# A graph network kernel: node one-hots of the end tiles made by one compare per 125 nodes over all neighbouring tiles of a side

## The reference: what is computed

```python
def _L1_gnn_ref(x, edge_index, W_interact, b_interact, W_update, b_update):
    src, dst = (edge_index[0], edge_index[1])
    h_edge = jnp.concatenate([x[src], x[dst]], axis=-1)
    m_ij = jax.nn.relu(h_edge @ W_interact + b_interact)
    m_i = jax.ops.segment_sum(m_ij, src, num_segments=x.shape[0])
    m_i = m_i / jnp.asarray(math.sqrt(AVG_DEGREE), dtype=x.dtype)
    out = x + jax.nn.relu((x + m_i) @ W_update + b_update)
    return out
```

## Time and profile before

| | |
|---|---|
| median of 3 runs | 1886.35 us (1883.08 to 1886.48) |
| span of the profiled execution | 1885.1 us, 1.25 us under that median |
| PE busy | 1694.0 us, 90% |
| DVE busy | 1432.5 us, 76% |
| ACT busy | 1037.5 us, 55% |
| POOL busy | 1024.9 us, 54% |
| edge stage | 1116 to 1885 us |

### The profile page before, as it was taken

The page is one execution under the profiler, slowest core; times in us unless marked ns, Lnnn a source line. Parts: engine busy times, 40 slices in busy tenths (PEclk is TensorE's granted clock), DMA queues, the critical chain, the costliest instruction groups (busy, mean ns, idle before and its releaser), DMA issues.

```text
span 1885.1 us, 45388 instructions
## 1 busy us (share of the span) xinstructions
PE 1694.0 (90%) x16778; PEld 1472.1 (78%) x16778; DVE 1432.5 (76%) x5527; ACT 1037.5 (55%) x2015; POOL 1024.9 (54%) x1075
## 2 busy tenths in 40 slices
PE   1606798999999979999999759999999999999998
PEld 1403676888778757777777649999999999999998
DVE  7968998999998335676653558888787777887776
ACT  1715575666667450000000248877777777777776
POOL 3364105656551004566551157777777777777775
PEclk9955999999999999999999879999999999999998
DMA  3005526465553656666666223443443444444442
GB/s 99 1 1 169 211 114 217 151 220 192 178 218 116 255 188 253 238 244 240 239 240 227 59 72 104 104 111 107 123 114 104 112 111 105 111 107 122 115 105 71
DMA packets 135014, 276.48 MB, mean 147 GB/s; under 512 B 21160, under 2 KB 82393, under 8 KB 134794
## 3 DMA queue, kind: packets, MB, share of 16 engines
q1 hardware_dynamic: 98427, 201.82, 31.1%
q0 software_dynamic: 34784, 71.17, 14.2%
q10 hardware_dynamic: 1584, 0.59, 0.1%
HBM read 192.26 MB, written 84.45 MB: 147 GB/s over the span
## 4 chain that ended last, share of the span: by engine, by line
PE 45%; DVE 24%; POOL 16%; issue 8%; DMA 4%; ACT 1%; POOLq 1%; SPq 1%; DVEq 0%
PE ps L1111 23%; POOL cells L810 8%; DVE hot L1595 7%; PE ps L1284 6%; PE ps L1277 5%; PE ps L1295 4%; POOL cell_lo L810 3%; POOL cell_hi L810 3%; DVE hot L1589 3%; PE ps L1097 2%; PE ps L1144 2%; DMA cells<-b_rows,work 2%; DVE keys L1685 1%; DVE keys L1619 1%; DVE keys L1684 1%
## 5 line engine op out<-in xcount | busy, mean ns | idle before, releaser
L1111 PE MATMUL ps<-slab,table 128*128 128x320 bf16 x4704 | 688.0, 300 | 2.5 <-DVE table L1834 2.4
L1111 PEld LDWEIGHTS ps<-slab,table 128*128 128x128 bf16 x4704 | 460.8, 98 | 167.9 <-DVE table L1834 2.9
L900 ACT ACTIVATE slab<-ps 128x980 bf16<-128x980 f32 x256 | 322.4, 1274 | 193.7 <-PE ps L1097 193.6
L810 POOL DMA_INDIRECT cells<-b_rows,work x336 | 319.9, 952 | 102.3 <-issue 96.9
L1284 PE MATMUL ps<-slab 125*128 125x128 bf16 x5496 | 357.1, 219 | 0.2 <-DVE slab L1917 0.2
L1284 PEld LDWEIGHTS ps<-slab 125*128 125x128 bf16 x5496 | 333.3, 98 | 4.8 <-DVE slab L1917 0.8
L1277 PE MATMUL ps<-table 125*128 125x128 f32 x1800 | 317.2, 286 | 1.7 <-DVE table L1911 1.7
L1005 ACT ACTIVATE lnw<-iota_w,keys 128x125 f32<-128x125 f32 x900 | 289.8, 389 | 1.6 <-POOL slab L801 1.6
L1277 PEld LDWEIGHTS ps<-table 125*128 125x128 f32 x1800 | 250.0, 192 | 1.9 <-issue 1.9
L1019 ACT ACTIVATE slab<-ps 128x384 f32<-128x384 f32 x300 | 146.1, 487 | 170.7 <-DVE ps L1926 167.6
L770 POOL DMA_INDIRECT hot<-t_rows,pairs x160 | 168.7, 1054 | 120.0 <-PE ps L1144 77.0
(11 more groups left out here) (304 smaller groups left out, 2144.6 us busy)
## 6 DMA issues: line engine op xcount, KB each, us to landing
slabs_d<-slab SPq DMA_DIRECT2D x16, 3920.0 KB, 12.9
slab<-slabs_d SPq DMA_DIRECT2D x16, 3920.0 KB, 14.4
hot<-lane_d SPq DMA_DIRECT2D x50, 576.0 KB
t_rows<-table SPq DMA_DIRECT2D x2, 4800.0 KB, 17.7
cells<-b_rows,work POOLq DMA_INDIRECT x336
inv<-inv_row SPq DMA_DIRECT2D x32, 160.0 KB
keys<-up_d SPq DMA_DIRECT2D x50, 96.0 KB
keys<-down_d SPq DMA_DIRECT2D x50, 96.0 KB
```

The costliest lines, as they stand in the source:

```text
L810: p.indirect_dma_start(rows_g[gi % RS][:, j, :], None, b_rows, bass.IndirectOffsetOnAxis(ap=node_t[:, t:t + 1], axis=0)).then_inc(e_gath[g ...
L900: a.activation(slab[par][:, :, u * UB * BW:(u + 1) * UB * BW].rearrange("p h (k d) -> p k h d", k=UB), psum_unit(u).rearrange("p k (h d) - ...
L1111: last = t.matmul(ps[:, 4 + par, 0:width], table[:, k // TERMS, k % TERMS, :], slab[par][:, k // TERMS, 0:width], start=k == 0, stop=k == ...
```

## The change

The windows of neighbouring tiles of a side overlap. Before, DVE compared each tile's 128 edges with each block of the tile's own window, 128 columns to a compare. After, a plan (`side_plan`) goes through the three tiles of a side; for each block of 125 nodes that a tile needs and no tile before it had, one compare covers this tile and those of the same side behind it that use the block too (128, 256 or 384 columns). The units lie one behind the other in a buffer for the side (19 units at most), one buffer for the low side in the place of the old one, one for the high side in `table`. They are kept until the next block of 125 source nodes comes to the same side. `HOTS` counts the batches, since some tiles then have nothing left to compare. The first group of a side has one more wait, on `e_sum`, for the old contents of its buffer. The matmuls are the same ones in the same order, with other addresses.

```diff
+    def side_plan(b, h):
+        tiles = range(SIDE) if h == 0 else range(TB - SIDE, TB)
+        at, made, unit = 0, [], {}
+        for first in tiles:
+            made.append([])
+            w0, w1 = window(b, first)
+            for w in range(w0, w1):
+                if (w, first) in unit:
+                    continue
+                shared = [t for t in tiles if t >= first and window(b, t)[0] <= w < window(b, t)[1]]
+                assert shared == list(range(first, first + len(shared)))
+                made[-1].append((w, first - tiles[0], len(shared), at))
+                for t in shared:
+                    unit[w, t] = at
+                    at += 1
+        return made, unit, at
...
-        end_hot = bt_all[:, o:o + 4 * MW * P].rearrange("p (s w e) -> p s w e", s=4, w=MW)
+        end_hot = [bt_all[:, o:o + UNITS3 * P], table[:, :, :, :].rearrange("p t k n -> p (t k n)")[
+            :, 2 * (NB * D + 4 * GW):2 * (NB * D + 4 * GW) + UNITS3 * P]]
...
-                        pe.wait_ge(e_endhot, gi + 1)
+                        pe.wait_ge(e_endhot, HOTS[gi])
...
-                                t.matmul(to, end_hot[0:BN, gi % 4, w - w0, :], bt[0:BN, at, k, :],
+                                t.matmul(to, end_hot[g // SIDE][0:BN, u:u + P], bt[0:BN, at, k, :],
...
-                at = end if end < SIDE else end - TB + GB
-                row = end_row[0:BN, b % 2, at * P:(at + 1) * P]
-                numbers = up_c if end < SIDE else down_c
-                for w in range(w0, w1):
-                    last = v.tensor_scalar(end_hot[0:BN, gi % 4, w - w0, :], row, numbers[0:BN, w:w + 1], None,
+                h = g // SIDE
+                if g % SIDE == 0 and gi >= GB:
+                    dve.wait_ge(e_sum, gi - SIDE)
+                numbers = down_c if h else up_c
+                for w, t0, n, at in SIDES[b, h][0][g % SIDE]:
+                    row = end_row[0:BN, b % 2, (h * SIDE + t0) * P:(h * SIDE + t0 + n) * P]
+                    last = v.tensor_scalar(end_hot[h][0:BN, at * P:(at + n) * P], row, numbers[0:BN, w:w + 1], None,
                                            ALU.is_equal)
-                last.then_inc(e_endhot, 1)
+                if SIDES[b, h][0][g % SIDE]:
+                    last.then_inc(e_endhot, 1)
```

13 lines of the change are left out of this document (11 added, 2 removed).

## The result

The changed kernel takes 1889.22 us (median of 20 runs, 1885.82 to 1892.18) against 1885.49 us for the kernel before (20 runs, 1883.08 to 1888.72). The ratio is 1.0019, with a 95% interval of 1.0013 to 1.0025. The changed kernel is slower by 3.7 us. 1885.0 us was forecast, with a range up to 1888.5, so the time lies 0.7 us above the range and on the other side of the kernel before. The loss is just inside the 0.2% that the prediction took as the least that can be told from no change, but with 20 runs of each the interval lies wholly above 1.

A forecast was written before the change was run, and what follows sets the result against it. POOL's chain of gathers was taken as the bound, PE 4.0 us behind. Profiled 1885.1 + 0 (semaphores) - 1.3 (gathers) + 0 (tail) = 1883.8 us; as median 1886.35 - 1.3 = 1885.0 us, range 1881.5 to 1888.5.

The forecast's parts named there:

- the side way: On POOL in the edge stage: DVE's compares lengthen gathers, and fewer compares were to save 1.3 us.
- The 0.13 us that I took as the price of a batch: POOL gathers beside DVE compares: a batch sometimes costs a gather up to 0.13 us, mostly nothing.
- a gain of up to 5.8 us, capped at 4.0 by PE: Rival: gathers get free of DVE; at most 5.8 us leave POOL's chain, PE binds after 4.0; 1882.3 us, chance 0.10.
- the chance of 0.81: Chance of the forecast's own case: DVE's work shrinks and the end of the edge stage stays.
- the wider compares hold gathers longer: Rival, first batch of each side: 100 batches each lengthen one gather by 0.13 us, 9.3 us more; 1895.6 us, chance 0.06.
- The bound: Edge stage: POOL issues one gather each 1.259 us without stopping and sets the end; PE is 4.0 us behind.
- DVE's saving: Compares in the edge stage: DVE's work falls from 302 to 210 us, saving 92 us, directly worth 0.
- The price of a wide compare: On DVE: 256-column compares at L1947 were to show a mean of about 0.30 us.
- The tail: From the last gather's end at 1873.4 us to 1885.1: no `prepare` in it, change 0.
- the three signs of being wrong: Mean gather outside 0.946 to 0.960 us, PE waits for L1947 in first batches, or POOL's gaps turning into waits.
- PE's wait for one-hots: PE's waits for node one-hots in the edge stage, 0.8 us in 3 waits, were to go; worth 0 on the end.
- The size of today's disturbance: Gathers spend 5.8 us above the median; 3.5 to 4 of it was put down to the compares.

The follow-up runs named there:

- e6_one: Kernel before with one 768-column compare for each of the 300 groups in place of its 1832 of 128 columns (one-hots wrong); ratio 1.0036.
- e1_split: Changed kernel, same plan, batches, buffers and order, with each 256- or 384-column compare written as two or three of 128; ratio to before 1.0011.
- e1_again: The same kernel as e1_split, run again; ratio to before 1.0001.
- e5_tt: Changed kernel with its compares made by `tensor_tensor` against a broadcast column instead of `tensor_scalar`; ratio to before 1.0319, 60.5 us slower.
- e4_none: Kernel before with node compares made for the first four groups alone, later groups using old one-hots (sums wrong); ratio 0.9998.
- e2_buffers: Changed kernel's two side buffers, but each tile's one-hots made in its own group with 128-column compares, as before; ratio to before 0.9994.
- f4_after_psum: Changed kernel with L1938 writing its sum back to PSUM and L1945 reading it there, on a slower chip; ratio to before 0.9995.

## Why the prediction was wrong

**The step that failed** is the one called the side way: of the compares' disturbance of gathers it took "-1.3 us, since the second and third batches get short and the nearest price of width is small". It measured +2.9 us in the sum of the gathers. I had let the disturbance go with the number of compares and, as the lower bound, with their columns, and had allowed for a loss with the width only in the range. e6_one shows that neither number nor DVE's time is what counts: 300 compares in place of 1832 lengthened the gathers by 3.8 us. e1_split and e1_again show it from the other side: with the same batches and buffers and 128 columns, the excess is 5.2 and 4.8 us in place of 7.3. What the runs showed in its place is a gather that waits for the end of the compare running 0.13 us after its start, so that the length of one compare counts and not their number.

The argument by which I made width cheap was that 118 more columns cost a compare only 0.03 us. That is true (0.036 us for 128 more), and it is a price per compare on DVE. For the gather, what changes is how many of them lose something: from 34 to 74 between 0.995 and 1.2 us. The 0.13 us that I took as the price of a batch was misread as well: at the start of the gather of the earlier trace rows the source compare L1911 is running, and the batch of node compares comes 0.18 us later.

**The range did not follow from its own bounds.** I gave a gain of up to 5.8 us, capped at 4.0 by PE, and a loss of about 4. Around 1886.35 us that is 1882.3 to 1890.4, which holds the measured 1889.22. The range as written took -3.5 and +3 around 1885.0, for which no row was given, and the chance of 0.81 was worked out for 1882.6 to 1890.1, a wider stretch on the slow side.

**The rival that came true** is "the wider compares hold gathers longer", to which I gave 0.06. Its direction was right, and its mechanism for a part: of the 40 more gathers between 0.995 and 1.2 us, 27 start during a node compare and 16 during L1939, with three fewer elsewhere. Its price was too high: I put 0.13 us on each of 100 gathers and 9.3 us in all.

**Right steps.** The bound: POOL's chain of gathers with no visible wait sets the end, and e5_tt bears it out, where 63.4 us more in the gathers came with 60.5 us more in the time. DVE's saving: 83.5 us of busy time against 92 us forecast, and its worth on the path was 0, as e4_none shows too, in which DVE lost nearly all compares and the ratio stayed at 0.9998. A part of the saving went back: L1937 and L1939, not touched by the change, take 0.008 and 0.014 us longer each, 6.6 us in all. Over the whole stage DVE waits 65 us longer for rows and 25 us longer for PE; the forecast had it all as waits for rows. The price of a wide compare was 0.298 us against "about 0.30". The new wait on `e_sum` shows nowhere. The tail kept its length. Of the three signs of being wrong, one came true, PE's waits for L1947 in first batches. The mean gather, 0.9585 us, stayed inside 0.946 to 0.960, so that sign was set too wide to show a loss of 3 us.

**Half right.** PE's wait for one-hots was to go; it grew from 0.8 to 3.5 us at the weight loads, in the high side's buffer, whose first batch has seven compares still and is now longer. Whether this adds to the end on top of the gathers isn't settled: 2.9 us in the gathers and 3.7 us (2.5 to 4.7 by the interval) in the medians are compatible with nothing from PE and with about a microsecond. The pairs with fewer gathers should have told it, and on their chips the times could not.

**The size of today's disturbance** was mis-sized as well: the node compares' part of the 5.8 us was taken as 3.7 and is about 2 us, by e4_none (4.6 to 2.4) and by the gathers that start beside them (1.9). The rule of the Trainium skill that I weighed ("SBUF — State Buffer", section "Who interferes with whom") says that whoever issues first holds the port pair for the whole instruction while the other fully blocks. I read it as if a whole batch held it, found no such wait and set it aside. It speaks of one instruction, and read so the traces agree with it in both directions: a gather waits for the end of the one instruction that was there first (1671.51 us in e6_one, 1.15 us), and one that starts 0.03 us behind the start of a compare goes undisturbed, while the compare takes longer (1589.62, 0.94 us); which of the two was first at the port in such a case the rows don't show. Whether these compares run in one of the two-port modes of which the rule speaks, no run here shows.

No complete kernel tried beats the kernel before: e2_buffers (0.9994) and f4_after_psum (0.9995) come nearest, both with intervals that reach above 1. The ones clearly below 1 leave gathers out.

## What to carry to other kernels

When one engine's chain without waits sets the time, ask of each edit on another engine whether it touches the duration of that chain's instructions, not only whether it waits. The mean against the median of its instructions and a count by length show it, and such a count in one execution can show what twenty timed runs barely tell. Then put each long instruction of the chain beside what runs on the other engine at its start: here that gave the price of a hit, what is left of the running instruction, where the counts alone only gave how many were hit. Merging DVE instructions into fewer and wider ones saves DVE time, and beside a chain of indirect DMAs it can cost more than it saves when DVE isn't the bound; an instruction with two operands in SBUF is the first that should be moved away from such a chain, by reading one operand from PSUM, and cutting it into pieces doesn't help.

## What the runs showed that I had not expected

- A gather on POOL gets through its first 0.13 us beside a `tensor_scalar` compare that was there before it, and then stands until that one compare ends: 0.08 us for a compare that ends 0.20 us after its start, 0.21 us for one that ends at 0.32. The compares behind it in the same batch don't hold it. A gather that starts within 0.06 us of the compare's start is mostly spared.
- A `tensor_tensor` compare with both operands in SBUF lengthened gathers to as much as 3.1 us and by 63.4 us in all; `tensor_scalar` compares of the same columns by 2.9 us. Five pieces of 128 columns in a row held a gather up for 0.78 us, up to 0.97 us in others.
- Ten instructions of 0.82 us (L1945) make up between nothing (e6_one) and 3.8 us (e4_none) of the gathers' time through gathers over 1.2 us, by chance of their place. That is as much as the change itself moved the time, and it hides or feigns small effects of other edits, as in e4_none.
- Chips differ: the same kernel before took 1886 us on some and 2158 to 2185 us on others, with gaps at PE that no wait explained.
